# One of 64 score blocks exponentiated by GpSimd and VectorE; router and token turns moved off TensorE

## The reference

```
h = h + attention(layernorm(h))      # 8 heads of 8; a bias per key column, made from the edges
h = h + moe(layernorm(h))
attention: softmax(q k^T / sqrt(8) + bias) v, heads joined, @ Wo + bo
moe(t):    p = softmax(t @ router_w^T); top 2 of 8, weights scaled to sum 1
           t + sum_e weight_e * (gelu(t @ w1[e] + b1[e]) @ w2[e] + b2[e])
```

## Time and profile before

| | us |
|---|---|
| three runs: median (lowest, highest) | 1132.17 (1129.41, 1133.17) |
| profiled execution | 1132.75 |
| its span, first to last instruction | 1130.7 |
| PE busy | 1086.5 (96%) |
| ACT busy | 1026.2 (91%) |
| DVE busy | 623.4 (55%) |
| POOL busy | 130.8 (12%) |

### The profile page before, as it was taken

One profiled execution on the slowest core, in us unless ns is written; L12 is line 12 of the kernel. 1 busy time (PEld: TensorE's weight loads), 2 busy tenths in 40 slices (PEclk: granted clock), 3 DMA queues, 4 the chain that ended last, 5 costly groups with the idle time before them and its releaser, 6 DMA issues.

```text
span 1130.7 us, 21748 instructions
## 1 busy us (share of the span) xinstructions
PE 1086.5 (96%) x7803; PEld 318.6 (28%) x7804; DVE 623.4 (55%) x1765; ACT 1026.2 (91%) x1127; POOL 130.8 (12%) x137
## 2 busy tenths in 40 slices
PE   3499999999999999999999999999999999999998
PEld 3122222222222222222222222222222222233333
DVE  8423465646464737374646465554646542476865
ACT  1299999999999999999999999999999999976654
POOL 3304011111111110102010101010101101000000
PEclk9899999999999999999999999999999999999999
DMA  2523131314141414241423232232323136049895
GB/s 55 128 59 67 55 85 46 88 41 109 30 119 31 107 43 105 46 105 46 104 46 95 56 94 56 74 76 66 84 58 76 42 85 152 16 136 241 236 246 164
DMA packets 73794, 100.78 MB, mean 89 GB/s; under 512 B 17276, under 2 KB 30076, under 8 KB 73660
## 3 DMA queue, kind: packets, MB, share of 16 engines
q1 hardware_dynamic: 71404, 98.73, 34.6%
q10 hardware_dynamic: 1776, 0.24, 0.1%
q0 software_dynamic: 480, 0.06, 0.1%
HBM read 57.67 MB, written 40.37 MB: 87 GB/s over the span
## 4 chain that ended last, share of the span: by engine, by line
PE 77%; ACT 10%; issue 6%; DVE 3%; DMA 2%; SPq 0%; ACTq 0%; POOL 0%; DVEq 0%; POOLq 0%
PE psum L1653 37%; PE psum L1637 21%; ACT probs L1369 10%; PE psum L1706 4%; PE psum L1730 4%; PE psum L743 2%; DMA m_cT<-cT_d 2%; PE psum L731 1%; PE psum L747 1%; PE psum L767 1%; PE psum L772 1%; PE psum L737 1%; PE psum L753 1%; PE psum L1716 1%; DMA x_d<-x2T 0%
## 5 line engine op out<-in xcount | busy, mean ns | idle before, releaser
L1369 ACT ACTIVATE probs<-psum 128x1024 f32<-128x1024 f32 x1024 | 941.1, 1241 | 26.5 <-PE psum L1637 26.4
L1653 PE MATMUL psum<-probs,VA 128*32 128x512 f32 x4096 | 547.0, 606 | 1.9 <-ACT probs L1369 0.4
L1637 PE MATMUL psum<-QA,KA 54*128 54x512 bf16 x2048 | 331.6, 385 | 8.4 <-issue 3.6
L1637 PEld LDWEIGHTS psum<-QA,KA 54*128 54x128 bf16 x2048 | 82.0, 93 | 484.9 <-ACT probs L1369 447.1
L1441 DVE STREAM_TRANSPOSE oT<-psum 128x512 f32<-128x512 f32 x64 | 45.9, 717 | 202.3 <-PE psum L1653 201.8
L1653 PEld LDWEIGHTS psum<-probs,VA 128*32 128x32 f32 x4096 | 81.8, 108 | 151.9 <-issue 130.9
L1404 ACT ACTIVATE probs<-psum,b 128x1024 f32<-128x1024 f32 x64 | 68.1, 1111 | 41.0 <-PE psum L1706 40.9
L1706 PE MATMUL psum<-m_x,w 64*128 64x512 f32 x256 | 61.6, 596 | 2.9 <-DMA m_cT<-cT_d 2.7
L1548 DVE TENSOR_TENSOR probs<-probs,psum 128x1024 f32<-128x1024 f32 x32 | 39.1, 1220 | 33.8 <-PE psum L1716 31.1
L1730 PE MATMUL psum<-probs,w 128*64 128x512 f32 x240 | 57.3, 598 | 0.0
L1308 POOL TENSOR_TENSOR p_rstd<-p_ve,neg_half 128x8 f32<-128x8 f32 x16 | 32.9, 2055 | 207.2 <-DVE p_ve L468 207.2
(11 more groups left out here) (180 smaller groups left out, 813.6 us busy)
## 6 DMA issues: line engine op xcount, KB each, us to landing
H_all<-comb_d SPq DMA_DIRECT2D x64, 256.0 KB, 5.5
QA<-q_parts_d SPq DMA_DIRECT2D x64, 192.0 KB
KA<-k_parts_d SPq DMA_DIRECT2D x64, 192.0 KB
q_parts_d<-qk_parts SPq DMA_DIRECT2D x32, 192.0 KB, 2.5
k_parts_d<-qk_parts SPq DMA_DIRECT2D x32, 192.0 KB, 2.7
xT<-in_xT SPq DMA_DIRECT2D x16, 256.0 KB, 2.7
q_parts_d<-qk_parts SPq DMA_DIRECT2D x32, 128.0 KB, 2.6
k_parts_d<-qk_parts SPq DMA_DIRECT2D x32, 128.0 KB, 2.5
```

Of the source, the lines that this page charges most:

```text
L1369: nc.scalar.activation(probs[:, k % PROB_BUFS, :], score_buf(buf_of(k)), ACT.Exp).then_inc(exped, 1)
L1637: last = pe.matmul(score_buf(buf_of(k))[:, (g % 2) * BANK:(g % 2 + 1) * BANK], KA[rows_of(h, SCORE_ROWS), h // 2, jt * P:(jt + 1) * P], QA ...
L1653: last = pe.matmul(o_acc[32 * g:32 * g + 32, :], VA[:, jt, h, :], probs[:, k % PROB_BUFS, (g % 2) * BANK:(g % 2 + 1) * BANK], start=(jt == ...
```

## The change

`SIDE_QUADS = (15,)`: the second half of quad 15 (two tiles) is no longer one of ACT's blocks. There are 63 blocks left, three buffers turn evenly and `buf_of`, `last_use` go. The two tiles are computed as helper steps side_0 and side_1 in slots 0 and 1; DVE drains them scaled by log2 e; POOL adds a rounding constant; DVE takes the fraction and shifts the rounded number's bits into an exponent (power of two); POOL evaluates a polynomial of degree five in the fraction in eight passes, four before the layer norm's power and four behind it; DVE multiplies the two in slot 15. `values(b, 15)`, in slot 17, reads the result.

norm_t and post_t leave PE: DVE transposes 32 x 32 blocks (`turn_normal`, `turn_x2`), four DMAs store them to DRAM in order, one loads them back. The router is four products with w_router as the held side, turned back by DVE. `combB` is stored by one DMA, and L1242 reads it in pieces of 512 bytes where there were 2048. The helper steps get other slots, and SP's, POOL's and DVE's bodies another order.

```diff
+SIDE_QUADS = (15,)
+EXPS = [(q, half) for q in range(QUADS) for half in range(2) if not (half and q in SIDE_QUADS)]
-AUX_SLOTS = {0: ("qk0", 0), 2: ("qk0", 1), 4: ("out_proj", 0), 6: ("out_proj", 1), 8: ("qk1", 0), 10: ("qk1", 1),
-             12: ("post_t", 0), 14: ("router", 0), 16: ("router", 1), 18: ("sq", 0), 19: ("embed", 0), 22: ("embed", 1),
-             24: ("v", 0), 26: ("v", 1), 28: ("combine_t", 0), 30: ("norm_t", 0)}
+AUX_SLOTS = {0: ("side_0", 0), 1: ("side_1", 0), 2: ("qk0", 0), 4: ("qk0", 1), 5: ("out_proj", 0), 7: ("out_proj",
+             1), 10: ("qk1", 0), 12: ("qk1", 1), 16: ("sq", 0), 18: ("router", 0), 21: ("embed", 0), 23:
+             ("embed", 1), 26: ("v", 0), 28: ("v", 1), 30: ("combine_t", 0)}
+FRACTION_SLOTS, POWER_SLOTS = (3,), (15,)
-CENTRE_SLOT, SCALE_SLOT, SPLIT_SLOT, SHIFT_SLOT, LEAD_SLOT, NORM_SLOT = 6, 10, 13, 20, 23, 28
+CENTRE_SLOT, SCALE_SLOT, SPLIT_SLOT, SHIFT_SLOT, LEAD_SLOT, NORM_SLOT = 8, 10, 14, 20, 24, 25
-COMBINE_SLOT, WEIGH_SLOT = 19, 22
+COMBINE_SLOT, WEIGH_SLOT = 21, 27
-G_SLOT = 26
+G_SLOT = 11
...
+            def side_round(b, side):
...
+                g.tensor_scalar(side_n[:, :], side_y[:, n % 2, :], 1.0, ROUNDER, ALU.mult, ALU.add).then_inc(side_rounded, 1)
+            def side_terms(b, side, first, last):
...
+                        g.tensor_scalar(side_p[:, :], side_p[:, :], 1.0, POWER_TERMS[c], ALU.mult,
+                                        ALU.add).then_inc(side_chain, 1)
+                    g.wait_ge(side_chain, base + 2 * (4 - c) + 1)
+                    g.tensor_tensor(side_p[:, :], side_p[:, :], side_f[:, :], ALU.mult).then_inc(side_chain, 1)
+                    g.wait_ge(side_chain, base + 2 * (4 - c) + 2)
...
+            def side_fraction(b, side):
...
+                v.scalar_tensor_tensor(side_f[:, :], side_n[:, :], ROUNDER, side_y[:, n % 2, :], ALU.subtract,
+                                       ALU.subtract).then_inc(side_split, 1)
...
+                v.tensor_scalar(side_y[:, n % 2, :].bitcast(I32), side_n[:, :].bitcast(I32), 23, None,
+                                ALU.logical_shift_left).then_inc(side_ready, 1)
+            def side_product(b, side):
...
+                v.wait_ge(side_chain, SIDE_CHAIN * (n + 1))
+                v.scalar_tensor_tensor(side_n[:, :], side_p[:, :], POWER_TERMS[0], side_y[:, n % 2, :], ALU.add,
+                                       ALU.mult).then_inc(side_done, 1)
...
@@ POOL's body @@
+                    side_round(b, 0)
+                    if b:
+                        g.wait_ge(pv_done, QUADS * b)
+                        alone(g)
+                        copy_v(1)
                     add_bo(b)
+                    side_terms(b, 0, 4, 3)
                     if b:
                         post_pow(b - 1)
+                    side_terms(b, 0, 2, 1)
...
@@ SP's body @@
+                    if b:
+                        store_x2(b - 1)
+                        load_x2(b - 1)
                     if b + 1 < NB:
                         all_parts(b + 1)
...
+                    if b + 2 < NB:
+                        store_normal(b + 2)
                     if b:
                         sp.wait_ge(aux_drained, aux_count(b, "combine_t"))
                         store_combine(b - 1)
                         store_weights(b - 1)
+                        store_tokens(b - 1)
+                    if b + 2 < NB:
+                        load_normal(b + 2)
...
                 def values(b, q):
...
+                    if q in SIDE_QUADS:
+                        pe.wait_ge(side_done, SIDES * b + SIDE_QUADS.index(q) + 1)
```

More of the change, by code:

```diff
@@ L41 @@
 QUADS = 2 * 2 * NCH
-BLOCKS = 2 * QUADS
+SIDE_QUADS = (15,)
+SIDES = len(SIDE_QUADS)
+EXPS = [(q, half) for q in range(QUADS) for half in range(2) if not (half and q in SIDE_QUADS)]
+EXP_OF = {place: k for k, place in enumerate(EXPS)}
+BLOCKS = len(EXPS)
+HALF_BLOCKS = EXP_OF[QUADS // 2, 0]
 GROUPS = 4
@@ L67 @@
 COMB_COPIES = ((0, 24), (24, 48), (48, 64))
-POST_UNITS = {2: "out_proj", 12: "post_t", 16: "router", 32: "combine_t"}
+POST_UNITS = {2: "out_proj", 16: "router", 32: "combine_t"}
 STATS_UNITS = {4: range(NCH // 2), 5: range(NCH // 2, NCH)}
@@ L241, in score_buf, with exp_at, exps_through, values_before @@
             return psum[:, 2 * BANK * i:2 * BANK * (i + 1)]
[L243 to L249, removed]
+        def exp_at(b, q, half):
+            return BLOCKS * b + EXP_OF[q, half]
+        def exps_through(b, q):
+            return exp_at(b, q, 0 if q in SIDE_QUADS else 1) + 1
+        def values_before(n):
+            return QUADS * (n // BLOCKS) + EXPS[n % BLOCKS][0] + 1
         o_acc = psum[:, 6 * BANK:7 * BANK]
@@ L740, in aux_step @@
                     rows = slice(D * int(step[-1]), D * int(step[-1]) + D)
+                    if step == "qk0" and n >= 2:
+                        pe.wait_ge(xn_loaded, 16 * (n - 1))
                     for i in halves:
                         cols = slice(i * BANK // 2, (i + 1) * BANK // 2)
-                        last = pe.matmul(aux[:, cols], w_qk[rows, :, :].rearrange("k a e -> k (a e)"), xnT[rows, cols],
+                        last = pe.matmul(aux[:, cols], w_qk[rows, :, :].rearrange("k a e -> k (a e)"), xnT[rows, n % 2, cols],
                                          start=True, stop=True)
@@ L746, in aux_step @@
                     for c in chunks:
-                        last = pe.matmul(aux[:, c * P:(c + 1) * P], xnT[:, c * P:(c + 1) * P],
+                        last = pe.matmul(aux[:, c * P:(c + 1) * P], xnT[:, n % 2, c * P:(c + 1) * P],
                                          w_v[:, :, :].rearrange("k t e -> k (t e)"), start=True, stop=True)
-                elif step == "post_t":
-                    pe.wait_ge(x2_made, n + 1)
-                    alone(pe)
-                    for c in range(NCH // 2):
-                        last = pe.transpose(aux[:, c * P:(c + 1) * P],
-                                            x2[:, c, :, :].rearrange("p t d -> p (t d)"), ident[:, :])
                 elif step == "sq":
@@ L763, in aux_step @@
                                              squares[:, i * BANK:(i + 1) * BANK], start=True, stop=True)
+                elif step in SIDE:
+                    i = SIDE.index(step)
+                    q = SIDE_QUADS[i // 2]
+                    h, ih, jt = 4 * (q // 16) + 2 + i % 2, q // 8 % 2, q % 8
+                    rows = slice(HALF_ROWS * (h % 2), HALF_ROWS * (h % 2) + SCORE_ROWS)
+                    last = pe.matmul(aux, KA[rows, h // 2, jt * P:(jt + 1) * P],
+                                     QA[rows, h // 2, ih * BANK:(ih + 1) * BANK], start=True, stop=True)
                 elif step == "out_proj":
@@ L1421, in _ @@
                     if u == ROUTER_UNIT:
-                        router_exp(END + POST.index("router") + 1)
+                        router_exp(NB - 1)
             @block.vector
             def _(v):
-                chain, _, _, (lead_step, lead_centre, normalise), prep_step, (shift_of, flag_of), rest = vector_steps(v)
+                chain, _, _, lead, prep_step, (shift_of, flag_of, side_step, side_fraction, side_product), rest = vector_steps(v)
+                lead_step, lead_centre, _, turn_normal = lead
                 split_low = rest[2]
                 post_step, tokens_steps, rank_steps, weigh_steps = vector_post(v)
-                measure_tokens, spread_tokens, centre_tokens, scale_tokens, add_tokens, turn_tokens = tokens_steps
+                measure_tokens, spread_tokens, centre_tokens, scale_tokens, turn_x2, add_tokens, turn_tokens = tokens_steps
                 share_experts, compare_above, compare_equal, break_ties, add_ties, rank_experts = rank_steps
@@ L1587, in _ @@
                         scale_tokens(NB - 1)
+                        turn_x2(NB - 1)
                     if u == ADD_UNIT:
```

299 lines of the change are left out of this document (195 added, 104 removed).

## The result

The changed kernel takes 1185.35 us (median of four runs, 1179.93 to 1194.73), the kernel before 1131.95 beside it. The ratio is 1.0481 (95%: 1.0437 to 1.0524): 4.8% slower. The profiled execution took 1185.4, its span 1183.6. The forecast was 1161, with a range up to 1178: the direction is right, the size 24 us too small. The four runs lie 15 us apart (granted clock 0.970 to 0.983), where those of the kernel before lie 4 apart; what follows is the account of the one profiled execution.

A forecast was written before the change was run, and what follows sets the result against it. ScalarE was taken as the bound, TensorE 0.4 us an image below it. From 1132.75, -13.6 for the removed block and +42 for collisions gave 1161 us; the range ran from 3 us beneath 1119 to 1178.

The forecast's parts named there:

- What bounds the kernel: Attention stage: ScalarE sets the pace, blocks 0.904 us apart in an image of 58.80; TensorE is 0.4 below it.
- What comes off: Attention image: ScalarE does 63 blocks; without collisions 57.95 us, 0.85 less, so -13.6 over 16 images.
- GpSimd's passes: Polynomial over 1024 columns: 2.35 us per two-input multiply, 1.05 per scale-and-add, four pairs 14.8 an image.
- The walk: Op-by-op timeline of an attention image: VectorE and GpSimd collide, TensorE's waits total 3.7; 3.0 taken, +42 over 14 images.
- the lead: Attention slots: 0.3 us subtracted from the 3.3 collision delay, leaving 3.0 an image.
- The variant in which casts don't collide: Same walk, VectorE keeping its turn over back-to-back ops and its casts not colliding: delay 1.7 us instead of 3.7.
- Edits at nothing: The change's other edits, such as added VectorE work and x2 and xn through DRAM, taken as costing 0.
- the xn load: xn through DRAM, landed 61.1, wanted 62.1 in the next image's slot 2: range 0 to +14, 0 taken.
- The expert stage at 0: Expert stage: -1.4 from post_t and router against up to +5 from shorter weight-row pieces; 0 taken.
- The cover holds: Rival in the attention stage: side_done is there by 30.85, no collision cost, 1119 us; chance 0.27.
- GpSimd first: Rival in the attention stage: GpSimd keeps its turn through all four ops, 1192 us; chance 0.05.
- The xn wait: Part of the rival of a delay near break-even, by collisions or TensorE's slot 2 xn wait: 1126 to 1136; chance 0.10.

The follow-up runs named there:

- experiment 7: Changed kernel with SIDE_QUADS empty: ScalarE does all 64 blocks, no side work, the rest of the change kept; 1152.98 us, ratio 1.0178.
- experiment 1: Two variants of the changed kernel: GpSimd's eight polynomial passes over 8 columns (1135.15 us, 1.0027), or replaced by write-only fills of about the same length (1133.46 us, 1.0019).
- experiment 4: Changed kernel with add_tokens and turn_tokens moved back from slot 11 to slot 26; 1150.04 us, ratio 1.0156.
- experiment 6: Kernel of experiment 5 with the last image's x2 loaded three units later in the expert stage; 1139.49 us, ratio 1.0059.
- experiment 3: Kernel before the change with one edit: expert weight rows read in 512-byte pieces instead of 2048; 1140.61 us, ratio 1.0075.
- experiment 5: Kernel of experiment 4 with 2048-byte weight rows (eight stores), tokens stored before the combine_t wait and the xn load right behind; 1142.97 us, ratio 1.0084.

## Why the prediction was wrong

**What bounds the kernel**: right. ScalarE's blocks are still 0.904 apart where nothing waits, and with TensorE lightened alone the image stays at 58.80 (experiment 7).

**What comes off**: right. 57.95 was forecast for an image without collisions, 57.88 measured in both kernels of experiment 1.

**GpSimd's passes**: right. 2.35 and 1.05 were taken, 2.44 and 1.06 measured, the excess being collisions of its own.

**The walk**: right nearly to the step. Product at 34.5 forecast, 34.2 measured; wait before `values(15)` 2.6 forecast, 2.5 measured; at blocks 28 to 40 the loss was taken at 3.3 and is 3.4, the lead gives 0.3 back in both, and the image loses 3.0 forecast, 3.1 measured. Experiment 1 shows the mechanism, experiment 4 the price of one pair of ops. The variant in which casts don't collide falls (2.43 against 0.69).

**No term for the clock**: the step that failed most, 12.7 of the 24 us. The front of the document said that the clock plays no part, which was true before, and the walk carried a stall of ScalarE as if a stall of TensorE cost its own length only. A kernel that makes TensorE stand 2.5 us, image after image, paid again behind nine of these 14 stalls. No image of before held a wait of TensorE of this length, but its trace had the price. TensorE stands 3.6 us before image 0, and the granted clock is 0.50 from 47.3 to 57.5:

```profile
47.66 1.04 PE L1637 MATMUL psum<-QA,KA 54*128 54x512 bf16 x4 [3.63 <-issue]
...
52.60 1.93 PE L1653 MATMUL psum<-probs,VA 128*32 128x512 f32 x8
...
57.91 1.07 PE L1653 MATMUL psum<-probs,VA 128*32 128x512 f32 x8
```

A quad's values take 1.93 there in place of 1.07. With the stall of 3.7 that the walk had, this was a rival to be given a chance and a price.

**"Edits at nothing", the xn load**: 0 was taken of a range up to 14; 5.2 came. The cover was worked out as 1.0 with four token stores at 1.80 on SP's queue. Here is SP's queue behind image 8, and TensorE in slot 2 of the next:

```profile
601.57 2.89 SPq L425 DMA_DIRECT2D h_d<-h2B  x4
604.57 0.37 SPq L442 DMA_DIRECT2D xnT<-xn_d  x1
```

```profile
607.50 0.67 PE L875 MATMUL psum<-xnT,w_qk 64*128 64x256 f32 x2 [0.36 <-DMA xnT<-xn_d]
```

The four stores took 2.89 this time. They took 1.80 in every image before, and 1.9 to 3.7 in the changed kernel; the cover was eaten in eight of 14 images. What makes their issue longer is not shown. A cover of 1.0 that hangs on an issue time of another kernel is none in half the cases; half of the range would have been the better term.

**The expert stage at 0, "up to +5"**: 6.5 came (7.9 against a stage that gained the 1.4). The x2 turn through DRAM was priced in the attention stage only; in this stage it puts a wait for its own store on SP's queue, ahead of the tokens, and the fourth group behind it has 6.3 of the 6.5 (loading x2 later gave 3.5 back, experiment 6). The pieces were priced by a slip of the token loads; alone they cost 8.3, by late loads and TensorE's clock behind one of them (experiment 3). How much of the changed kernel's loss is theirs stays open: whole rows, bought with eight stores, did not shorten the stage (experiment 5).

**Rivals.** "The cover holds" fell to the reading ops, as forecast; "GpSimd first" fell too (the halves end between its ops). The xn wait was put down as a rival to the forecast where it was an addition to it. The range shut 7 us too low because the clock had no term and the other two were taken at nothing.

## What to carry to other kernels

When work is moved to an engine whose instructions and another's exclude each other, don't compare their idle times; walk the two timelines op by op, and look at every op that stands beside a reading pass, an 8-column one too. A wait of TensorE of 2.5 us cost its length and then, in nine of 14 cases here, another 1 to 2 us at half clock: give any such stall that a change creates a term of this kind. And count each load on a shared DMA queue with its issues at their worst, not their mean, and each wait of the queue for its own store with what is queued behind it: two such places ate here what the idea brought.

## What the runs showed of the hardware

- A fill on GpSimd (1052 ns over 1024 columns) does not delay VectorE's two-input ops (420 ns); a multiply of the same data does (up to 3.0 us for two halves). SBUF — State Buffer, "Who interferes with whom", of the Trainium skill says of a VectorE instruction with two inputs in SBUF that it contends with a GpSimd instruction that reads there, not with one that only writes; experiment 1 agrees.
- A one-input op of VectorE over 1024 columns was delayed by the fill too: a shift took 1522 ns in place of 694 (experiment 1).
- An op over 8 columns, `tensor_scalar`, was held up 1.6 us by a GpSimd pass.
- The granted clock fell to 0.50 around waits of TensorE of 2.5 us, for 3.4 or 6.8 us, in nine of 14 like images; in five the same wait left it at 1.00. It fell behind waits of 2.0 and 1.65 us in experiment 7 too, and behind none of the 42 waits of 1.5 to 1.7 us for the product in experiments 4 to 6. What decides between them is open.
- The same four stores of 64 KB took 1.8 us to issue on SP in every image of the kernel before and 1.9 to 3.7 in the changed one.
- The same bytes broadcast from DRAM in 512-byte pieces in place of 2048 cost 8.3 us in a stage in which DMA is busy 0.77 of the time (experiment 3).
